# Rotary halves swapped on VectorE instead of by two more projections, the sine's product on GpSimd

## What is computed

```python
def _apply_rope(t, cos, sin):
    t1, t2 = jnp.split(t, 2, axis=-1)          # the 8 columns of a head: first four, last four
    rot = jnp.concatenate([-t2, t1], axis=-1)
    return t * cos + rot * sin
def qkv(h):
    t = (h @ qkv_W).reshape(b, n, 3, H, HD)
    q, k, v = (t[:, :, 0], t[:, :, 1], t[:, :, 2])
    return (_apply_rope(q, cos, sin), _apply_rope(k, cos, sin), v)
...
self_out = _attn(q, k, v, attn_mask[None, None]).reshape(b, s, d) @ attn_out_W
x = x + g_msa * self_out
xc = _ln(x, normc_w) * (1 + sc_x) + sh_x       # cross-attention, MLP, L1, L2, L3 follow
```

## Time and profile before

| | |
|---|---|
| median of three runs | 1162.31 us |
| the profiled execution | 1166.16 us, its span 1164.4 us |
| mean granted TensorE clock | 0.963 |
| PE busy | 1058.0 us, 91% of the span |
| DVE busy | 780.5 us, 67% |
| ACT busy | 574.3 us, 49% |
| POOL busy | 653.5 us, 56% |
| DMA | 22.89 MB, mean 20 GB/s |

### The profile page before, as it was taken

One profiled execution on the slowest core, in us unless ns is written; L12 is line 12 of the kernel. 1 busy time (PEld: TensorE's weight loads), 2 busy tenths in 40 slices (PEclk: granted clock), 3 DMA queues, 4 the chain that ended last, 5 costly groups with the idle time before them and its releaser, 6 DMA issues.

```text
span 1164.4 us, 28612 instructions
## 1 busy us (share of the span) xinstructions
PE 1058.0 (91%) x11711; PEld 669.1 (57%) x11711; DVE 780.5 (67%) x1875; ACT 574.3 (49%) x803; POOL 653.5 (56%) x762
## 2 busy tenths in 40 slices
PE   7899999999998997998999679999999999999898
PEld 5445555556654775665567435665555556665476
DVE  5777777777884433666667668878888777777421
ACT  0034433456656553544445226666555566665553
POOL 5466666677775331211112568888687665577531
PEclk9799999999999997999999869999999999998999
DMA  4300000000000112000000000000000000000001
GB/s 176 126 5 2 11 20 11 11 20 21 11 20 20 39 35 85 6 12 6 6 6 12 6 12 7 2 2 2 1 3 1 2 2 2 2 2 2 2 28 46
DMA packets 9281, 22.89 MB, mean 20 GB/s; under 512 B 1392, under 2 KB 1648, under 8 KB 8768
## 3 DMA queue, kind: packets, MB, share of 16 engines
q1 hardware_dynamic: 9152, 21.07, 5.3%
HBM read 18.90 MB, written 2.15 MB: 18 GB/s over the span
## 4 chain that ended last, share of the span: by engine, by line
PE 67%; DVE 18%; issue 6%; POOL 4%; ACT 4%; DMA 0%; DVEq 0%; POOLq 0%; ACTq 0%
PE weighed L645 11%; DVE negmax L1116 10%; PE row_scores L587 6%; PE scores L791 5%; PE weighed L668 5%; PE scores L618 5%; PE scores L544 4%; PE quads L528 3%; PE row_scores L791 3%; PE quads L551 2%; PE quads L539 2%; ACT p L1515 2%; PE scores L658 2%; PE scores L630 2%; PE row_scores L802 2%
## 5 line engine op out<-in xcount | busy, mean ns | idle before, releaser
L1116 DVE TENSOR_REDUCE negmax<-row_scores 128x8 f32<-128x616 f32 (+1 forms) x312 | 300.7, 964 | 85.5 <-PE row_scores L587 63.0
L1515 ACT ACTIVATE p<-scores 128x1024 f32<-128x1024 f32 (+1 forms) x256 | 247.7, 1018 | 215.5 <-PE scores L630 215.5
L618 PE MATMUL scores<-qblk,work 32*77 32x512 f32 (+1 forms) x1280 | 205.7, 618 | 11.5 <-ACT p L1515 6.9
L1668 POOL TENSOR_TENSOR kblk_r<-work,pack_const 128x308 fp32r<-128x308 f32 (+1 forms) x160 | 134.0, 838 | 118.1 <-PE row_scores L587 102.3
L645 PE MATMUL weighed<-p,v 77*32 77x128 f32 (+1 forms) x5120 | 173.8, 277 | 2.5 <-DVE nat L1132 2.5
L587 PE MATMUL row_scores<-kblk_r,qr 32*128 32x308 f32 (+1 forms) x624 | 141.4, 442 | 37.3 <-DVE negmax L1116 36.6
L1658 POOL TENSOR_TENSOR qblk<-work,pack_const 128x512 f32<-128x512 f32 x160 | 166.2, 1039 | 0.0
L645 PEld LDWEIGHTS weighed<-p,v 77*32 77x32 f32 (+1 forms) x5120 | 130.6, 110 | 45.1 <-issue 42.7
L630 PE MATMUL scores<-nblk,select 32*77 32x512 f32 (+1 forms) x640 | 155.4, 798 | 0.0
L587 PEld LDWEIGHTS row_scores<-kblk_r,qr 32*128 32x128 f32 x624 | 63.4, 188 | 157.6 <-issue 77.7
L1132 DVE STREAM_TRANSPOSE nat<-weighed 128x256 f32<-128x256 f32 x160 | 71.1, 445 | 44.3 <-PE weighed L645 44.3
(11 more groups left out here) (289 smaller groups left out, 1852.1 us busy)
## 6 DMA issues: line engine op xcount, KB each, us to landing
shared<-gates_hbm SPq DMA_DIRECT2D x24, 256.0 KB, 3.2
shared<-in_ctx_tok SPq DMA_DIRECT2D x16, 154.0 KB
pack_w_l<-in_w_l SPq DMA_DIRECT2D x1, 2058.5 KB, 10.9
x<-in_x_tok SPq DMA_DIRECT2D x8, 256.0 KB, 6.4
out_x<-x SPq DMA_DIRECT2D x8, 256.0 KB, 2.0
layers_w<-in_w_l SPq DMA_DIRECT2D x1, 1289.0 KB, 7.8
ctxT<-in_ctxT SPq DMA_DIRECT2D x1, 1232.0 KB, 9.2
layers_w<-in_w_l SPq DMA_DIRECT2D x1, 640.0 KB, 6.6
```

Of the source, the lines that this page charges most:

```text
L618: mm = e.matmul(scores[0:nk, g, :], k_of[q % 3][at, s * nk:(s + 1) * nk], qblk[n % 2][at, :], start=layer.mask != "qk", stop=False, skip_g ...
L1116: e.tensor_reduce(negmax[q % 2][:, 2 * h:2 * h + 2, 0, s * NJ:(s + 1) * NJ], row_banks(n, h)[:, :, 0:NJ * nk].rearrange("p g (j k) -> p g ...
L1515: e.activation(p[n % 2][0:nk, 8 * h:8 * h + 8, :], scores[0:nk, 2 * h:2 * h + 2, :].rearrange("p g (j q) -> p (g j) q", j=NJ), ACT.Exp, bi ...
L1668: e.tensor_tensor(kblk_r[n % 2][:, 0:NJ * nk].rearrange("p (j k) -> p j k", j=NJ), k_of[q % 3][:, s * nk:(s + 1) * nk].unsqueeze(1).to_bro ...
```

## The change

The swapped projections are gone, with their weights, their PSUM bank and the waits on it. DVE multiplies the projection with the cosine as before and then copies it with partitions exchanged four apart (`stream_shuffle`, pattern i XOR 4 in each group of 32) from `quad_bank` into `rot`. POOL multiplies `rot` with the sine, and then adds, as before. The table `sin_live[:, which]` is the same that DVE used.

```diff
-    ("w_l0", [("l0_q", D), ("l0_qswap", D), ("l0_k", D), ("l0_kswap", D), ("l0_v", D), ("l0_o", D),
+    ("w_l0", [("l0_q", D), ("l0_k", D), ("l0_v", D), ("l0_o", D),
...
-            def project_q(q, early):
+            def project_q(q):
                 layer = layer_of(q)
                 w.wait_ge(L(layer.wq), 16)
                 xn_ready(q)
-                if layer.rope:
-                    w.wait_ge(exp_done, early)
-                    e.matmul(scores[:, 1, :], W["l0_qswap"], xn[q % 3], start=True, stop=True).then_inc(proj_swapped, 1)
                 e.matmul(quad_bank[:, :], W[layer.wq], xn[q % 3], start=True, stop=True).then_inc(proj_q, 1)
...
-                if layer.rope:
-                    w.wait_ge(exp_done, early)
-                    e.matmul(scores[:, 1, :], W["l0_kswap"], kv_source(q), start=True, stop=True).then_inc(proj_swapped, 1)
...
                 def scores_read(t):
-                    if cl == 0 and qi + 2 in quads and layer_of(qi + 2).rope:
-                        w.wait_ge(rope_half, 4 * (qi + 2) + 3)
...
-                    if cl == 3 and qi + 3 in quads and layer_of(qi + 3).rope:
-                        w.wait_ge(rope_half, 4 * (qi + 3) + 1)
...
                 w.wait_ge(dve_setup, DVE_AT["sin1"])
+                w.wait_ge(proj, q + 1)
                 w.wait_ge(*freed)
-                w.wait_ge(rope_done, 2 * (q - 1) + which + 1)
-                w.wait_ge(proj_swapped, 2 * q + which + 1)
-                e.tensor_tensor(by_seq(rot[which][:, :]), by_seq(scores[:, 1, :]),
-                                sin_live[:, live:live + 1, :].to_broadcast([128, QUAD, S]), ALU.mult).then_inc(rope_half, 1)
-                w.wait_ge(proj, q + 1)
                 e.tensor_tensor(by_seq(dst), by_seq(quad_bank[:, :]),
                                 cos_live[:, live:live + 1, :].to_broadcast([128, QUAD, S]), ALU.mult).then_inc(rope_half, 1)
+                w.wait_ge(rope_done, 2 * (q - 1) + which + 1)
+                e.stream_shuffle(rot[which][:, :], quad_bank[:, :], [i ^ (HD // 2) for i in range(TILE)]).then_inc(rope_half, 1)
...
             def add_rotated(q, which):
                 dst = (q_of, k_of)[which][q % 3]
                 w.wait_ge(rope_half, 4 * q + 2 * which + 2)
+                e.tensor_tensor(by_seq(rot[which][:, :]), by_seq(rot[which][:, :]),
+                                sin_live[:, which:which + 1, :].to_broadcast([128, QUAD, S]), ALU.mult).then_inc(rope_turned, 1)
+                w.wait_ge(rope_turned, 2 * q + which + 1)
                 e.tensor_tensor(dst, dst, rot[which][:, :], ALU.add).then_inc(rope_done, 1)
```

More of the change, by code:

```diff
@@ L278, in build @@
         raw_turned, raw_done = sem("raw_turned"), sem("raw_done")
-        proj_q, proj_k, proj_v, proj_swapped = sem("proj_q"), sem("proj_k"), sem("proj_v"), sem("proj_swapped")
+        proj_q, proj_k, proj_v, rope_turned = sem("proj_q"), sem("proj_k"), sem("proj_v"), sem("rope_turned")
         rope_half, rope_done, q_done, k_done = sem("rope_half"), sem("rope_done"), sem("q_done"), sem("k_done")
@@ L524, in project_q, with project_k @@
                 xn_ready(q)
-                if layer.rope:
-                    w.wait_ge(exp_done, early)
-                    e.matmul(scores[:, 1, :], W["l0_qswap"], xn[q % 3], start=True, stop=True).then_inc(proj_swapped, 1)
                 e.matmul(quad_bank[:, :], W[layer.wq], xn[q % 3], start=True, stop=True).then_inc(proj_q, 1)
-            def project_k(q, early):
+            def project_k(q):
                 layer = layer_of(q)
@@ L722, in quad_work @@
                     if cl == 0 and qi + 2 in quads:
-                        project_k(qi + 2, early)
+                        project_k(qi + 2)
                     if cl == 1 and qi + 3 in quads and layer_of(qi + 3).name == "l3c":
@@ L731, in quad_work @@
                     if cl == 3 and qi + 3 in quads:
-                        project_q(qi + 3, early)
+                        project_q(qi + 3)
                 for t in range(4 * lo + first, end):
@@ L1880, in _constants @@
             "rope_sin": sin, "ones": np.ones((128, 128), np.float32)}
-def _swap(w):
-    return w.reshape(w.shape[0], NH, 2, HD // 2)[:, :, ::-1].reshape(w.shape[0], D)
 def _col(v):
@@ L1908 @@
     wq, wk, wv = (z("L0", "qkv_W")[:, c * D:(c + 1) * D] for c in range(3))
-    p["l0_q"], p["l0_qswap"], p["l0_k"], p["l0_kswap"] = wq, _swap(wq), wk, _swap(wk)
+    p["l0_q"], p["l0_k"] = wq, wk
     p["l0_v"], p["l0_o"] = (wv), _by_tile(z("L0", "attn_out_W"))
```

## The result

The changed kernel takes 1158.05 us, the median of ten runs (1154.9 to 1159.8), beside 1162.94 for the kernel before (ten runs, 1160.51 to 1166.21). The ratio is 0.9961, 95% interval 0.9945 to 0.9976: 4.5 us faster by the ratio, 2.8 to 6.4. I had forecast a gain of 9.3 us and 1153.0. The sign is right and the time is within the range, but about half of the gain is missing.

A forecast was written before the change was run, and what follows sets the result against it. PE led, its chain alternating with DVE's negmax. Six q slots x 0.78, five k slots x 0.86, 0.5 for t = 0 and -0.2 for the ramp gave 9.3 us: median 1162.31 to 1153.0, range 1150 to 1158.5.

The forecast's parts named there:

- the freed 0.86: PE time a dropped projection frees on the chain: 1.06 + 0.86 - 1.05, taken as 0.86 us.
- Q slot 0.78: Full pipeline, q slots: next negmax starts 0.78 us earlier, DVE becoming the limit by a little; PE alone would allow 0.86.
- k slot 0.86: Full pipeline, k slots: gain of 0.86 us, set by PE; DVE would allow 1.13.
- t = 0 0.51: First k slot, with no weighted sum yet: gain of 0.51 us.
- The shuffle, the product, POOL's cover at `attn`: DVE shuffle 0.69 us (at most 0.90); POOL's sine product 1.27; attn ready 0.1 to 0.7 us before DVE wants it, cost 0.
- rival 3: Dear shuffle on DVE ahead of negmax: no gain at 1.45 us, 1166 median at 1.7 us; chance 0.06.
- rival 2: POOL becomes the limit: nothing gained (1162) at about 2.1 us a product; chance 0.09, including gains lost between engines.
- The ramp: Start of first attention: row scores 1.65 us later, mostly regained by dropping L527; DVE's negmax slips about 0.2, counted as -0.2.
- the slot t = -1: Last q slot of the ramp: gains 0.78 us like the other q slots.
- from there DVE is the limit for some 10 us, so the 0.2 is carried: From the negmax at 37.32, DVE limits with the same number of instructions, so the 0.2 us slip neither grows nor shrinks.
- then the chain loses L527, 1.71 us: Ramp, behind the first row scores: dropped projection saves 1.71 us at half clock, leaving PE where it was, 0.06 ahead.
- Rival 1: The ramp pays: PE stays at 1.2 GHz through the next projection, GpSimd may slow DVE; price 3 to 5 us, 1157; chance 0.21.

The follow-up runs named there:

- pipe_old: Changed kernel with only the ramp's three q and two k slots shuffled, the full pipeline as in the kernel before: 1164.54 us, ratio 1.0030 to before.
- ramp_old: Changed kernel with the two projections and DVE's sine product kept in the ramp's three q and two k slots: 1154.69 us, ratio 0.9937 to before.
- after: The changed kernel itself, as first measured and profiled: 1158.05 us, ratio 0.9961 to the kernel before.
- a2: The changed kernel run and profiled again without any edit: 1158.04 us, ratio 0.9959 to the kernel before.
- own_bank: Changed kernel with quad 0's k projection written to the second scores bank instead of the shared quad_bank: 1157.95 us, ratio 0.9943 to before.
- q0_shuf: Changed kernel with quad 0 by two projections and DVE's sine product, other quads shuffled with shuffle ahead of cosine product: 1153.45 us, ratio 0.9915 to before.
- b2: The kernel before, run and profiled again without any edit: 1161.37 us, ratio 0.9997 to the kernel before.
- old_q12: Changed kernel with two projections and DVE's sine product in q slots of quads 1 and 2 and k slot of quad 1: 1158.27 us, ratio 0.9959.
- ramp_fill: Changed kernel with one extra, unread matmul behind each projection in the ramp's three q and two k slots: 1157.76 us, ratio 0.9961 to before.
- old_q0: Changed kernel with two projections and DVE's sine product kept for quad 0 alone: 1154.85 us, ratio 0.9926 to before.
- own_bank_sine: Changed kernel with quad 0's k projection in the second scores bank and quad 0's sine products on DVE: 1155.36 us, ratio 0.9924 to before.
- dve_sine: Changed kernel with the ramp's sine products on DVE behind the shuffle instead of on GpSimd: 1157.56 us, ratio 0.9958 to before.

## Why the prediction was right in the pipeline and wrong in the sum

- **What bounds the kernel, and the freed 0.86.** Right. The chain in the k slots lost the second projection, nothing else.
- **Q slot 0.78, k slot 0.86, t = 0 0.51.** Measured 0.81, 0.85 and 0.50. Five of each and t = 0 were to give 8.7 us up to the end of the stretch; the stretch gave 8.9 to 9.0, in every profile with a shuffled pipeline.
- **The shuffle, the product, POOL's cover at `attn`.** 0.73, 1.27, and 0.6 us of waiting in all, as before. Right in the pipeline; rival 3 falls, and rival 2 as far as a dearer product goes.
- **The ramp: the step that failed.** I had forecast -0.2 for it and 0.78 for the slot t = -1, so +0.6. By the medians it costs 2.65 us (pipe_old) to 3.35 (ramp_old). That, some 3 to 4 us, is most of the difference between 9.3 and the 4.5 to 4.9 measured; the rest is within the intervals. Two steps of the forecast are at fault.
- **The first: "from there DVE is the limit for some 10 us, so the 0.2 is carried".** Up to there the given pair went as forecast, counted from the first projection. I expected the row scores 1.65 us later, and they start 25.56 - 13.43 = 12.13 us behind it, where it was 26.55 - 16.11 = 10.44: 1.69. The chain then lost L527, and the fourth `negmax`, at 37.32 in the earlier trace rows and at 34.89 now, comes at 21.46 instead of 21.21: 0.25 late, and I had 0.2. But the eighth comes at 32.54 instead of 30.79, 1.75 late, and the twelfth 0.86 late, where I had it 0.58 early. Timeline of DVE after, and in the last row the eighth `negmax` before:

```profile
34.89 1.21 DVE L1104 TENSOR_REDUCE negmax<-row_scores 128x8 f32<-128x1024 f32 x1
...
44.69 0.55 DVE L1052 TENSOR_TENSOR p<-weighed,p 32x384 f32<-32x384 f32 x1 [1.41 <-PE weighed L485]
...
45.97 1.22 DVE L1104 TENSOR_REDUCE negmax<-row_scores 128x8 f32<-128x1024 f32 x1 [0.54 <-PE row_scores L581]
...
46.90 1.20 DVE L1116 TENSOR_REDUCE negmax<-row_scores 128x8 f32<-128x1024 f32 x1
```

  DVE waits for PE, and PE had waited 1.27 us for `kblk_r` and 1.01 for `xh` (above), which stand behind quad 1's products on GpSimd: POOL works without a gap from 35.07 to 44.99. From 41 us on PE's granted clock is 0.50 (1.2 GHz) besides. I had let GpSimd's lateness end with the first row scores and put its cost for quad 1 at nothing. From the seventh to the eighth `negmax` after, a2, pipe_old and own_bank take 4.2 to 4.5 us and q0_shuf 3.3; all others take 2.4. But these five reach the seventh 14.4 to 14.5 us behind the first, and the others, b2 (13.3) apart, in 15.5 to 16.9. So the waits are where the time is lost, and not all of it is a loss; old_q12, which has none of them, is no faster. What limits the later ramp when they are gone is open.
- **The second: "then the chain loses L527, 1.71 us".** That price is L527 at half clock in one execution. In b2, the same kernel, the granted clock is 1.00 from 30 to 40 us and the same pair takes 1.02 (last section); its fourth `negmax` comes at 17.01, its twelfth at 41.91, 4.3 us ahead of a2's 46.23. How much the dropped projection pays back thus hangs on the clock of the execution, and I took it from the dearer one. The first quad's 1.7 us, on the other hand, is in every profile with that quad as in the changed kernel: 13.5 to 13.7 us to the first `negmax` instead of 11.1 to 11.9.
- **Rival 1, the ramp pays** (1157, a chance of 0.21). Its place and its time were right; that its 1157 is near the median is luck, since its mechanism was not: it had the clock stay low for want of matmuls through the next projection, but that one, L533 at 35.66, takes 1.02 us at full clock in after, and ramp_fill, with the matmuls back, gained nothing that can be measured. One of its signs stays open, PE's longer idle time at the first row scores: from 24 to 33 us the mean granted clock is 0.50 to 0.64 in the nine profiles with the first quad shuffled, 0.62 to 0.64 in four of the five others, and 1.00 in b2. Whether the longer wait keeps the clock low, no run here separates. The mask's product, L1036 in the earlier trace rows with 1.20 us, which was to get slower, takes 0.80 in a2 and 0.85 in after (and 1.49 in b2).

## What to carry to other kernels

A cost that a full pipeline hides has to be added up once more in the ramp, at every place where the engine stands in the chain and not at the first alone: there GpSimd's 1.27 us products counted in full for quad 0, and in the changed kernel's profiles again for quad 1. Treat "it is late, but then it saves as much" as two terms with two chances, above all where the saving was read in one execution. Where a change is worth it in the loop only, keep the old form for the first iteration (old_q0 here: one condition).

## What else the runs showed

**A long wait that is worth nothing.** In a2 PE waits 2.40 us for the shared `quad_bank` ahead of the first k projection. own_bank took that wait away and the first `negmax` did not move (13.54 us, 13.57 in a2), since GpSimd had its 7.52 us of work to do all the same.

**DVE and GpSimd in each other's way.** In own_bank_sine the first two `xh` rows took 1.52 and 1.33 us, where they take 1.04 in after. Beside the first ran this DVE product with both inputs in SBUF (timeline of DVE), beside the second two of DVE's casts:

```profile
21.41 0.69 DVE L1092 TENSOR_TENSOR rot<-rot,sin_live 128x512 f32<-128x512 f32 x1
```

DVE's row keeps its 0.69 us; here GpSimd pays, where in the earlier trace rows DVE did (1.20), and in dve_sine too (1.26). In these rows the one that started second paid: DVE at 21.41 and GpSimd at 21.48 here, GpSimd at 20.93 and DVE at 21.26 in dve_sine. The Trainium skill (SBUF - State Buffer, Who interferes with whom) has such a pair take turns on a shared port. The trace agrees on the first row, a loss of 0.48 us on GpSimd's side, and shows 0.29 more beside the casts.

**TensorE at half pace with the clock granted in full.** In b2's stretch from 16 to 20 us (columns as the earlier trace rows) the granted clock is 1.00 (2.4 GHz), yet the pair of projection matmuls takes 2.05 us, which in the ramp's later rows takes 1.02:

```profile
16.00:20.00 4.00, 3.64 (x6) 1.19 (x5) 1.77 (x6) 0.00 (x0) 0.00 (x0) 1.00 0.16 59
```

```profile
16.04 2.05 PE L527 MATMUL scores<-work,layers_w 128*128 128x512 f32 x2
...
30.20 1.02 PE L527 MATMUL scores<-work,layers_w 128*128 128x512 f32 x2
```

The granted clock in the rows is thus not all that sets TensorE's pace at the start of a program. Why, no run here shows.
